# A graph network's edge passes: row numbers kept in place, gathers written out, other rings

## Chip, cores, metric

One core of a Trainium2 chip. The metric is the time of one execution on the device in microseconds; lower is better. Everything is float32.

## What is computed

Four graph layers, one after the other, over 6,250 nodes of 128 features and 100,000 edges. Each layer first takes `h = relu(layernorm(x))` and adds its result to `x`. Cut to what matters:

```python
# first: a message per edge, chosen by its type t of 4, then a GRU over the nodes
h_e = relu([x[src], x[dst]] @ W1[t] + b1[t]);  m = (h_e @ W2[t] + b2[t]) * sigmoid([x[src], x[dst]] @ aw[t] + ab[t])
agg = zeros.at[dst].add(m);  x = layernorm(GRU(agg, x) + x)
# second: attention of every node (row src) over its neighbours (dst)
att = softmax over the edges of a row of (tanh(x)[dst] @ a);  out = segment_sum(tanh(x)[dst] * att, src)
# third: eight bases, mixed by the edge's relation of 64
msg = sum_b w_comp[rel, b] * (x[src] @ weight[b]) * edge_weight;  out = relu(segment_sum(msg, dst) + bias + x @ loop)
# fourth: three graph convolutions
out = segment_sum((x @ W)[src] * norm, dst) + b
```

## The kernel before

**Tables and tiles.** The kernel first sorts the edges by target node (and a second time by source, for the second layer): every edge gets a slot in one of `TILES` = 832 tiles of 128 edges, and all edges of a tile point into one window of 128 nodes (50 windows). A slot holds eight numbers as float32 (`slots`, 128 x tiles x 8): the row of the source node, the rows in the first layer's tables, keys, relation and weight. GpSimd (POOL) scatters them to their slots with indirect DMAs (`Scatter`, L195), and `load_slots` (L669) loads the sorted table into on-chip memory, where it stays.

Each layer then has a table stage, which computes a row per node and stores it in the chip's main memory, and an **edge pass**, which brings the row of each edge's source back and sums over a tile's edges with a matmul against a 0/1 matrix (`onehot`). All passes share one frame. Tiles are handled in groups of `G` = 4, in a ring of `R` = 4 slots (`R1` = 8 in the second layer). `for_groups` (L446) writes out the first turn of the ring, loops over the middle turns (`Fori`), and writes out the last. Each engine runs its own program of this form, and semaphores tie them.

**A gather.** POOL issues one indirect DMA per tile: 128 rows, one per partition, whose numbers are read as int32 from on-chip memory. Since the slots hold floats, ACT first copies the group's numbers into a small int32 ring `index` ("stage"), and POOL waits for it, then issues the group's gathers:

```python
def restage(g, slot, turn):                      # ACT, fourth layer, L1641
    act.wait_ge(q["product"], g + 1)
    stage(g + R, slot)
def gather(g, slot, turn):                       # POOL, L1623
    pool.wait_ge(q["staged"], g + 1)
    pool.sem_inc(q["turns"], 1)
    for j in range(G): pool.indirect_dma_start(...)
```

So the numbers of group g + 4 are staged, and its gathers issued, once PE has done group g's product and the slot is free.

**The passes.** *First layer* (`edges0`, L699): two gathers per tile (L743, tables of 528-byte rows), DVE adds the two rows (L786), ACT makes the message (L766, L769) and then stages (L751), PE multiplies with a 128 x 512 onehot (L846), DVE adds the result into the window's sum (L810); beside it the edge's eight mixing coefficients for the third layer are worked out (L855, L863, L818, L825). *Second layer* (`edges1`, L1075): one gather per tile (L1118), then a running softmax through ACT, PE and DVE four steps deep; ACT stages at the end of `scale_sums` (L1129 called at L1163). Its first staging stands behind the semaphore `cleared`, which DVE raises after clearing the sums (L1176). *Third layer* (`edges2`, L1399): one gather per tile of a 4 KB row, the source's eight products (L1429). ACT scales four of the eight (L1453); DVE scales two in one instruction (L1476), folds two more in one after the other (`chain`, L1488), builds the onehot (L1465), and adds the group before the last into the sums (L1498); PE multiplies the onehot with the six parts left (L1521). ACT's order is: scale group k, then wait for the product of group k - 1 and stage (L1437). DVE's chain of group g waits for the product of group g - 2. *Fourth layer* (`edges3`, L1609), three times: one gather of 512-byte rows per tile (L1628), onehot (L1655), one matmul per tile (L1676), one addition per tile (L1665); ACT does nothing but stage (L1636).

DVE reads the window numbers of a group into registers before its additions (`load_windows_of`, L685).

Of the kernel before, what the change touches and what calls it, by code (L numbers as in the profile page):

```python
# [21 lines left out]
I32 = mybir.dt.int32  # L22
# [21 lines left out]
G, R, R1 = 4, 4, 8  # L44
STEP = G * R1
# [421 lines left out]

def flat(ap):

    return ap.rearrange("p a f -> p (a f)")  # L470
# [198 lines left out]
def load_slots(nc, D, K):  # L669

    with Scope(nc, "slots") as s:
        loaded, cleared = s.sem("loaded"), s.sem("cleared")
# [12 lines left out]
def load_windows_of(nc, K, side, g, before=0):  # L685
# [13 lines left out]
def edges0(nc, A, D, K, acc):  # L699


    with Scope(nc, "edge0") as s:
        index = s.sb("index", [P, R, G, 2], I32)
# [10 lines left out]
        q = {n: s.sem(n) for n in ("loaded", "cleared", "staged", "turns", "summed", "scored", "hidden_done", "onehot_done",  # L714
# [20 lines left out]
        @block.gpsimd  # L735
        def _(pool):
            def gather(g, slot, turn):

                pool.wait_ge(q["staged"], g + 1)
                pool.sem_inc(q["turns"], 1)  # L740
                for j in range(G):
                    for f, (rows, table) in enumerate(((rows_s, "tab_src"), (rows_d, "tab_dst"))):
                        pool.indirect_dma_start(out=rows[:, slot, j, :], out_offset=None, in_=D[table][:, :],  # L743
                                                in_offset=bass.IndirectOffsetOnAxis(ap=index[:, slot, j, f:f + 1], axis=0)).then_inc(gathered[slot], 16)

            for_groups(pool, [(0, gather)])

        @block.scalar
        def _(act):
            def stage(g, slot):  # L750
                act.activation(index[:, slot, :, :], slots[:, ds(g * G, G), F_SRCT:F_DSTT + 1], ACT.Copy).then_inc(q["staged"], 1)  # L751

            for r in range(R):
                stage(r, r)

# [5 lines left out]
            def hide(g, slot, turn):  # L761
# [9 lines left out]

                act.wait_ge(q["hidden_done"], g + 1)
                stage(g + R, slot)
# [301 lines left out]
def edges1(nc, D, K, acc):  # L1075
# [5 lines left out]
    with Scope(nc, "edge1") as s:  # L1081
        slots = s.sb("slots", [P, TP, SF])
        index = s.sb("index", [P, R1, G, 1], I32)
# [16 lines left out]
        q = {n: s.sem(n) for n in ("loaded", "cleared", "staged", "turns", "other_done", "score_done", "score_turned",  # L1100
# [10 lines left out]
        @block.gpsimd  # L1111
        def _(pool):
            def gather(g, slot, turn):

                pool.wait_ge(q["staged"], g + 1)
                pool.sem_inc(q["turns"], 1)
                for j in range(G):
                    pool.indirect_dma_start(out=rows[:, slot, j, :], out_offset=None, in_=D["tab1"][:, :],  # L1118
                                            in_offset=bass.IndirectOffsetOnAxis(ap=index[:, slot, j, 0:1], axis=0)).then_inc(gathered[slot], 16)

            for_groups(pool, [(0, gather)], R1)

        @block.scalar
        def _(act):
            act.wait_ge(q["loaded"], 16)
            act.wait_ge(q["cleared"], 1)

            def stage(g, slot):
                act.activation(index[:, slot, :, :], slots[:, ds(g * G, G), 0:1], ACT.Copy).then_inc(q["staged"], 1)  # L1129

            for r in range(R1):
                stage(r, r)
# [17 lines left out]
            def scale_sums(g, slot, turn):  # L1150
# [11 lines left out]

                stage(g + R1, slot)  # L1163
# [235 lines left out]
def edges2(nc, D, K, acc):  # L1399
# [3 lines left out]

    VB = BASES // 2
    LINKS = 1 + G * (VB - 2)
    PARTS = [0, 1, *range(VB, BASES)]
    with Scope(nc, "edge2") as s:
        index = s.sb("index", [P, R, G, 1], I32)
# [4 lines left out]
        q = {n: s.sem(n) for n in ("loaded", "staged", "turns", "onehot_done", "chain", "scaled", "product", "added")}  # L1413
# [9 lines left out]
        def _(pool):  # L1423
            def gather(g, slot, turn):

# [9 lines left out]
        def _(act):  # L1435
# [3 lines left out]
            for r in range(R):  # L1439
                stage(r, r)  # L1440
# [168 lines left out]
def edges3(nc, D, K, layer, acc):  # L1609

    with Scope(nc, f"edge3_{layer}") as s:
# [22 lines left out]
        def _(act):  # L1634
# [3 lines left out]
            for r in range(R):  # L1638
                stage(r, r)
# [153 lines left out]
```

## Time and profile before

| | us |
|---|---|
| median of 3 timed runs | 11041.12 |
| lowest, highest | 11011.58, 11056.96 |
| span of the profiled execution | 13468.9 |

| stretch of the profiled execution | from, to (us) |
|---|---|
| sorting, first scatters, first tables | 0 to 1775 |
| first layer's edge pass | 1775 to 4664 |
| update, scatters for the second layer | 4664 to 6354 |
| second layer's edge pass | 6354 to 7767 |
| third layer's tables, edge pass | 7767 to 8009, to 9473 |
| fourth layer, three edge passes | 9583 to 10806, 10894 to 12112, 12193 to 13426 |

The page gives each engine's busy time over the span (PE: matmul, PEld: its weight load, DVE, ACT, POOL, SP). A queue name with a q (SPq, ACTq) stands for instructions of an engine's own sequencer, such as register moves, which don't count as busy. POOL's busy time in an indirect DMA is the making of its descriptors; the data move afterwards. "Issue" is idle time in which an engine waited for nothing that the trace shows. A releaser is inferred from semaphore events, and one name may stand for another where a semaphore was used again: in the third and fourth layer "DMA slots_s<-sort_zero" and "DMA tab_dst<-tab_ob" as releaser of DVE and ACT stand for the product's semaphore. The profiled execution took 13,468.9 us; the timed ones are executions of the same program without a profile.

### The profile page before, as it was taken

Reading aid. Unit: us, or ns where it says so; the run is one execution under the profiler, and the core shown is the slowest. Engines: PE = TensorE matmul, PEld = TensorE weight load, DVE = VectorE, ACT = ScalarE, POOL = GpSimd, SP = SyncE. Lnnn points to the kernel's source line nnn. Section 1 sums busy time; section 2 is a strip of 40 time slices with the busy share of each in tenths; the row PEclk is TensorE's granted clock in tenths of the full one; section 3 lists DMA queues with packets and bytes.
Section 4 is the critical chain, followed back from the end, with each engine's and each line's share of the span. In section 5 each row is a group of like instructions: output and inputs, shape, how many; then the busy total and the mean of one; then the engine's idle time right before and its main releaser. Section 6 shows DMA issues by size and latency. Waiting matters only on the chain. (4 is left out here: it accounts for less than half of the span.)

```text
span 13468.9 us, 135567 instructions
## 1 busy us (share of the span) xinstructions
PE 5832.8 (43%) x31462; PEld 5005.1 (37%) x31462; DVE 5298.2 (39%) x11470; ACT 2648.3 (20%) x8918; POOL 7546.1 (56%) x7650
## 2 busy tenths in 40 slices
PE   0003545565565511371444468888433333333332
PEld 0001235555454511251444447787322222222222
DVE  7801034444454400013555546666432332233233
ACT  1000011111111100011555536776200000000000
POOL 2476655655566566406555525555466656665665
PEclk9998567766776755555666689999655555555555
DMA  9901111111111200001111148888211121121112
GB/s 18 13 7 46 51 51 40 41 41 39 40 40 41 36 2 2 1 0 31 39 40 39 39 155 297 298 298 297 79 44 44 45 44 45 45 44 45 45 44 47
DMA packets 587395, 879.08 MB, mean 65 GB/s; under 512 B 340739, under 2 KB 377041, under 8 KB 586828
## 3 DMA queue, kind: packets, MB, share of 16 engines
q0 software_dynamic: 329728, 772.96, 20.9%
q1 hardware_dynamic: 257612, 105.52, 8.7%
q8 instruction: 18, 0.29, 0.0%
q14 instruction: 37, 0.30, 0.0%
HBM read 791.80 MB, written 86.16 MB: 65 GB/s over the span
## 5 line engine op out<-in xcount | busy, mean ns | idle before, releaser
L1628 POOL DMA_INDIRECT edge_rows<-tab,edge_index x2496 | 2399.8, 961 | 1286.1 <-issue 739.4
L1676 PE MATMUL edge_psum<-edge_rows,edge_onehot 128*128 128x128 f32 x4992 | 1250.5, 429 | 2461.3 <-DVE edge_onehot L1655 1434.8
L1676 PEld LDWEIGHTS edge_psum<-edge_rows,edge_onehot 128*128 128x128 f32 x4992 | 1076.8, 318 | 2634.7 <-issue 1507.1
L846 PE MATMUL edge_psum<-edge_hidden,edge_onehot 128*128 128x130 f32 x6656 | 1148.4, 338 | 1297.0 <-DVE acc_acc L810 940.4
L1665 DVE TENSOR_TENSOR acc_acc<-acc_acc,edge_psum 128x128 f32 x2496 | 716.5, 287 | 2514.2 <-remote 1334.2
L846 PEld LDWEIGHTS edge_psum<-edge_hidden,edge_onehot 128*128 128x128 f32 x6656 | 1034.7, 242 | 1416.1 <-DVE acc_acc L810 987.9
L743 POOL DMA_INDIRECT edge_rows_s<-tab_src,edge_index x832 | 842.0, 1012 | 938.6 <-ACT edge_index L751 700.5
L1521 PE MATMUL edge_p_m<-edge_rows,edge_onehot 128*128 128x128 f32 x9984 | 1199.7, 282 | 286.8 <-ACT edge_rows L1453 217.8
L1521 PEld LDWEIGHTS edge_p_m<-edge_rows,edge_onehot 128*128 128x128 f32 x9984 | 1165.8, 197 | 320.7 <-DVE acc_acc L1498 273.6
L1429 POOL DMA_INDIRECT edge_rows<-tab,edge_index x832 | 840.1, 1010 | 639.0 <-ACT edge_index L1437 432.9
L1118 POOL DMA_INDIRECT edge_rows<-tab,edge_index x832 | 797.6, 959 | 626.0 <-ACT edge_index L1129 377.8
L743 POOL DMA_INDIRECT edge_rows_d<-tab_dst,edge_index x832 | 862.4, 1037 | 264.8 <-issue 264.8
L1453 ACT ACTIVATE edge_rows<-edge_rows,edge_coef 128x128 f32<-128x128 f32 x3328 | 996.8, 390 | 33.9 <-issue 17.2
L810 DVE TENSOR_TENSOR acc_acc<-acc_acc,edge_psum 128x520 f32 x832 | 577.7, 694 | 971.7 <-remote 658.1
L1636 ACT ACTIVATE edge_index<-all_slots 128x4 int32 (+1 forms) x636 | 129.0, 208 | 3585.7 <-remote 1664.3
L195 POOL DMA_INDIRECT slots_s<-upd_pay_ring,upd_row_ring x656 | 630.8, 962 | 314.9 <-issue 270.9
L1276 PE MATMUL edge_p_u<-edge_rows,edge_prob 128*128 128x129 f32 x1664 | 375.0, 395 | 751.1 <-ACT edge_prob L1169 511.5
L1276 PEld LDWEIGHTS edge_p_u<-edge_rows,edge_prob 128*128 128x128 f32 x1664 | 319.4, 286 | 819.9 <-ACT edge_prob L1169 507.6
L195 POOL DMA_INDIRECT slots_d<-sort_pay_ring,sort_row_ring x320 | 385.2, 1204 | 257.4 <-DMA sort_pay_ring<-pay_d 158.0
L990 DVE TENSOR_TENSOR upd_new<-upd_rz,upd_p_g 128x128 f32<-128x128 f32 x50 | 14.4, 288 | 1266.1 <-issue 715.6
L195 POOL DMA_INDIRECT slots_d<-tab_pay_ring,tab_row_ring x400 | 384.2, 961 | 226.0 <-issue 143.6
L794 DVE TENSOR_TENSOR edge_onehot<-all_iota,all_slots 128x1024 f32<-128x1024 f32 x416 | 507.6, 1220 | 0.0
(253 smaller groups left out, 9556.9 us busy)
## 6 DMA issues: line engine op xcount, KB each, us to landing
edge_rows<-tab,edge_index POOLq DMA_INDIRECT x4160
tab<-tab_o SPq DMA_DIRECT2D x50, 512.0 KB, 2.6
edge_rows_s<-tab_src,edge_index POOLq DMA_INDIRECT x832
edge_rows_d<-tab_dst,edge_index POOLq DMA_INDIRECT x832
tab_src<-tab_oa SPq DMA_DIRECT2D x50, 264.0 KB
tab_dst<-tab_ob SPq DMA_DIRECT2D x50, 264.0 KB
slots_s<-upd_pay_ring,upd_row_ring POOLq DMA_INDIRECT x656
tab<-acc_own SPq DMA_DIRECT2D x15, 640.0 KB, 3.6
```

The source lines that it names most:

```text
L195: pool.indirect_dma_start(out=self.table[:, :], out_offset=bass.IndirectOffsetOnAxis(ap=self.row_ring[:, z, j:j + 1], axis=0), in_=self.pa ...
L743: pool.indirect_dma_start(out=rows[:, slot, j, :], out_offset=None, in_=D[table][:, :], in_offset=bass.IndirectOffsetOnAxis(ap=index[:, sl ...
L810: v.tensor_tensor(at, at, psum[:, j % 2, :, 0:2 * SW], ALU.add).then_inc(q["added"], 1)
L846: m = pe.matmul(psum[:, j % 2, t // 2, (t % 2) * SW:(t % 2) * SW + SW], onehot[:, slot % 2, j, t * P:(t + 1) * P], hidden[:, slot % 2, j, ...
L1118: pool.indirect_dma_start(out=rows[:, slot, j, :], out_offset=None, in_=D["tab1"][:, :], in_offset=bass.IndirectOffsetOnAxis(ap=index[:, s ...
L1276: m = pe.matmul(p_u[:, z, j // 2, (j % 2) * HW:(j % 2) * HW + H + 1], prob[:, z, j, :], rows[:, slot, j, 0:H + 1], start=True, stop=True)
L1429: pool.indirect_dma_start(out=rows[:, slot, j, :], out_offset=None, in_=D["tab2"][:, :], in_offset=bass.IndirectOffsetOnAxis(ap=index[:, s ...
L1453: a = act.activation(part, part, ACT.Copy, scale=coef[:, ds(G * g + j, 1), b])
L1521: m = pe.matmul(at, onehot[:, z, j, :], rows[:, slot, j, b * H:(b + 1) * H], start=(n == 0), stop=(n == len(PARTS) - 1))
L1628: pool.indirect_dma_start(out=rows[:, slot, j, :], out_offset=None, in_=D[f"tab3_{layer}"][:, :], in_offset=bass.IndirectOffsetOnAxis(ap=i ...
L1665: v.tensor_tensor(at, at, psum[:, slot % 2, j * P:(j + 1) * P], ALU.add).then_inc(q["added"], 1)
L1676: m = pe.matmul(psum[:, slot % 2, j * P:(j + 1) * P], onehot[:, slot % 2, j, :], rows[:, slot, j, :], start=True, stop=True)
```

## The change

1. `load_slots` turns three of the slots' eight fields into int32 **in place**, on DVE, in one instruction each; the second layer's own slots are turned by one ACT instruction. `index` and all staging are gone.
2. A helper `gather_groups` issues all gathers of a pass from a Python loop, so that POOL's program is written out without a loop. Before a group it waits directly for what frees the slot: the message made (first layer), the sums' product (second), the product (third and fourth).
3. The third layer works in groups of two tiles with a ring of eight (same memory); its sums now go two per group.
4. The fourth layer's ring has eight slots of four tiles instead of four. The title's "ring of eight" stands for both.

```diff
+R3 = 8
+G2, R2 = 2, 8
...
+def index_of(slots, field):
+
+
+    return slots[:, 0:TILES, field].bitcast(I32)
+
+
+def gather_groups(pool, ring, freed, gathered, parts, G=G):
+
+
+    for g in range(TILES // G):
+        slot = g % ring
+        wait(pool, freed, g - ring + 1)
+        for j in range(G):
+            for rows, table, slots, field in parts:
+                index = slots[:, G * g + j, field:field + 1].bitcast(I32)
+                pool.indirect_dma_start(out=rows[:, slot, j, :], out_offset=None, in_=table[:, :],
+                                        in_offset=bass.IndirectOffsetOnAxis(ap=index, axis=0)).then_inc(gathered[slot], 16)
...
+            v.wait_ge(loaded, 16)
+            for field in (F_SRC, F_SRCT, F_DSTT):
+                v.tensor_copy(index_of(K["slots"], field), K["slots"][:, 0:TILES, field]).then_inc(indexed, 1)
...
-            for_groups(pool, [(0, gather)])
+            gather_groups(pool, R, q["hidden_done"], gathered,
+                          [(rows_s, D["tab_src"], slots, F_SRCT), (rows_d, D["tab_dst"], slots, F_DSTT)])
...
-                act.wait_ge(q["hidden_done"], g + 1)
-                stage(g + R, slot)
...
-            for_groups(pool, [(0, gather)], R1)
+            pool.wait_ge(q["indexed"], 1)
+            gather_groups(pool, R1, q["sums"], gathered, [(rows, D["tab1"], slots, 0)])
...
+            act.activation(index_of(slots, 0), slots[:, 0:TILES, 0], ACT.Copy).then_inc(q["indexed"], 1)
             act.wait_ge(q["cleared"], 1)
...
-                stage(g + R1, slot)
...
+    G, R, GROUPS = G2, R2, TILES // G2
...
+            gather_groups(pool, R, q["product"], gathered, [(rows, D["tab2"], slots, F_SRC)], G)
...
-            def restage(g, slot, turn):
-
-                act.wait_ge(q["product"], g + 1)
-                stage(g + R, slot)
...
-            for_groups(act, [(0, scale), (1, restage)])
+            for_groups(act, [(0, scale)], R, GROUPS)
...
-                        if sums and (j == 0 or (b, j) == (VB - 1, G // 2)):
+                        if sums and j == 0:
...
-        rows = s.sb("rows", [P, R, G, H])
+        rows = s.sb("rows", [P, R3, G, H])
...
+            gather_groups(pool, R3, q["product"], gathered, [(rows, D[f"tab3_{layer}"], slots, F_SRC)])
...
-            for_groups(v, [(-1, hots), (0, accumulate)])
+            for_groups(v, [(-1, hots), (0, accumulate)], R3)
...
-            "pool_sems": [s.ctx.enter_context(nc.semaphore(f"pool_dma{n}")) for n in range(5 * R + R1)],
+            "pool_sems": [s.ctx.enter_context(nc.semaphore(f"pool_dma{n}")) for n in range(R + R2 + 3 * R3 + R1)],
```

## Rows read from the trace of the kernel before

**Rows 1.** The page: span, and busy time of each engine (share of the span).
```profile
span 13468.9 us, 135567 instructions
...
PE 5832.8 (43%) x31462; PEld 5005.1 (37%) x31462; DVE 5298.2 (39%) x11470; ACT 2648.3 (20%) x8918; POOL 7546.1 (56%) x7650
```

**Rows 2.** Busy time by stretch; columns: us, engines, PEclk, DMA share, GB/s.
```profile
1775.00:4664.00 2889.00, 1626.22 (x9817) 1471.85 (x9818) 1342.59 (x1843) 391.83 (x1439) 1704.36 (x1664) 0.70 0.18 40
...
8009.00:9473.00 1464.00, 1184.72 (x9854) 1151.17 (x9855) 970.64 (x2876) 1018.94 (x3500) 840.11 (x832) 0.97 0.88 299
...
9583.00:10806.00 1223.00, 413.68 (x1648) 356.05 (x1648) 374.52 (x1028) 42.00 (x206) 795.15 (x832) 0.52 0.19 44
```

**Rows 3.** What POOL waited for; columns: us in total, times, longest.
```profile
POOL edge_rows_s L743 <- ACT edge_index L751: 700.5, 77, 19.9
POOL edge_rows L1628 <- ACT edge_index L1636: 546.7, 152, 8.0
...
POOL edge_rows L1429 <- ACT edge_index L1437: 432.9, 193, 16.2
POOL edge_rows L1118 <- ACT edge_index L1129: 377.8, 87, 11.8
```

**Rows 4.** POOL in order of time, fourth layer's first pass; start, us.
```profile
10227.90 0.94 POOL L1628 DMA_INDIRECT edge_rows<-tab,edge_index  x1 [0.30 <-issue]
10229.15 0.94 POOL L1628 DMA_INDIRECT edge_rows<-tab,edge_index  x1 [0.30 <-issue]
...
10236.65 0.94 POOL L1628 DMA_INDIRECT edge_rows<-tab,edge_index  x1 [0.30 <-issue]
10242.11 0.94 POOL L1628 DMA_INDIRECT edge_rows<-tab,edge_index  x1 [4.51 <-ACT edge_index L1636]
```

**Rows 5.** All engines in order of time, the same stretch.
```profile
10224.23 2.07 PE L1676 MATMUL edge_psum<-edge_rows,edge_onehot 128*128 128x128 f32 x8 [3.69 <-DMA edge_rows<-tab,edge_index]
...
10229.40 2.07 PE L1676 MATMUL edge_psum<-edge_rows,edge_onehot 128*128 128x128 f32 x8 [3.10 <-DMA edge_rows<-tab,edge_index]
...
10241.11 1.58 DVE L1665 TENSOR_TENSOR acc_acc<-acc_acc,edge_psum 128x128 f32 x4 [12.15 <-DMA tab_dst<-tab_ob]
10241.11 0.41 ACT L1636 ACTIVATE edge_index<-all_slots 128x4 int32 x2 [14.54 <-DMA tab_dst<-tab_ob]
```

**Rows 6.** Who waited for one line: the fourth layer's table product L1587.
```profile
  DVE acc_own L1604: 62.0, 145
```

**Rows 7.** Line L174 on SP: durations min/median/max in ns.
```profile
L174 SPq MOVE upd_pay_ring<-pay_s x80: 3/700/1400, 4711.1 to 5597.0; - x80
...
L174 SPq MOVE sort_pay_ring<-pay_d x38: 29/29/29, 639.1 to 1017.4; - x38
```

**Rows 8.** All engines in order of time, start of the fourth layer's first pass.
```profile
9581.82 0.50 ACT L1636 ACTIVATE edge_index<-all_slots 128x4 int32<-128x4 f32 x4 [5.99 <-PEq L86]
9582.84 0.98 POOL L1628 DMA_INDIRECT edge_rows<-tab,edge_index  x1 [7.99 <-ACT edge_index L1636]
...
9584.13 0.95 POOL L1628 DMA_INDIRECT edge_rows<-tab,edge_index  x1 [0.31 <-issue]
```

**Rows 9.** The same at the start of the second layer's pass.
```profile
6346.99 5.43 DVE L1176 MEMSET acc_acc<- 128x6450 f32 x1 [1.29 <-issue]
```

**Rows 10.** Groups by line: DVE instructions over 784 numbers.
```profile
L350 DVE SCALAR_TENSOR_TENSOR sort_picked<-sort_win,all_iota,sort_scan 128x784 f32<-128x784 f32 x100 | 103.0, 1031 | 0.1
...
L385 DVE TENSOR_SCALAR sort_mask<-sort_win,all_iota 128x784 f32 x100 | 53.9, 628 | 0.7 <-DVE sort_row L427 0.4 <-DVE sort_payd L380 0.3
```

**Rows 11.** All engines in order of time, third layer, steady stretch.
```profile
8720.99 1.23 DVE L1476 TENSOR_TENSOR edge_rows<-edge_rows,edge_coef 128x1024 f32<-128x1024 f32 x1 [2.30 <-DMA slots_s<-sort_zero]
...
8725.42 0.29 DVE L1498 TENSOR_TENSOR acc_acc<-acc_acc,edge_p_m 128x128 f32 x1
...
8726.14 5.62 PE L1521 MATMUL edge_p_m<-edge_rows,edge_onehot 128*128 128x128 f32 x48 [1.36 <-ACT edge_rows L1453]
...
8735.06 1.22 DVE L1476 TENSOR_TENSOR edge_rows<-edge_rows,edge_coef 128x1024 f32<-128x1024 f32 x1 [2.41 <-DMA slots_s<-sort_zero]
```

More of the change, by code:

```diff
@@ L1412, in edges2 @@
         p_m = s.ps("p_m", [P, 2, 512])
-        q = {n: s.sem(n) for n in ("loaded", "staged", "turns", "onehot_done", "chain", "scaled", "product", "added")}
+        q = {n: s.sem(n) for n in ("loaded", "onehot_done", "chain", "scaled", "product", "added")}
         gathered = [K["pool_sems"].pop() for _ in range(R)]
@@ L1423, in _ @@
         def _(pool):
-            def gather(g, slot, turn):
-                pool.wait_ge(q["staged"], g + 1)
-                pool.sem_inc(q["turns"], 1)
-                for j in range(G):
-                    pool.indirect_dma_start(out=rows[:, slot, j, :], out_offset=None, in_=D["tab2"][:, :],
-                                            in_offset=bass.IndirectOffsetOnAxis(ap=index[:, slot, j, 0:1], axis=0)).then_inc(gathered[slot], 16)
-            for_groups(pool, [(0, gather)])
+            gather_groups(pool, R, q["product"], gathered, [(rows, D["tab2"], slots, F_SRC)], G)
         @block.scalar
         def _(act):
-            def stage(g, slot):
-                act.activation(index[:, slot, :, :], slots[:, ds(g * G, G), F_SRC:F_SRC + 1], ACT.Copy).then_inc(q["staged"], 1)
-            for r in range(R):
-                stage(r, r)
             act.wait_ge(q["loaded"], 16)
-            def restage(g, slot, turn):
-                act.wait_ge(q["product"], g + 1)
-                stage(g + R, slot)
             def scale(g, slot, turn):
@@ L1522, in products @@
                 m.then_inc(q["product"], 1)
[L1524 removed]
+            for_groups(pe, [(0, products)], R, GROUPS)
 def finish2(nc, A, D, K, acc):
@@ L1611, in edges3 @@
     with Scope(nc, f"edge3_{layer}") as s:
[L1612 to L1613 removed]
+        rows = s.sb("rows", [P, R3, G, H])
         onehot = s.sb("onehot", [P, 2, G, P])
         psum = s.ps("psum", [P, 2, 512])
[L1616 to L1617 removed]
+        q = {n: s.sem(n) for n in ("cleared", "onehot_done", "product", "added")}
+        gathered = [K["pool_sems"].pop() for _ in range(R3)]
         block = s.block()
@@ L1622, in _ @@
         def _(pool):
-            def gather(g, slot, turn):
-                pool.wait_ge(q["staged"], g + 1)
-                pool.sem_inc(q["turns"], 1)
-                for j in range(G):
-                    pool.indirect_dma_start(out=rows[:, slot, j, :], out_offset=None, in_=D[f"tab3_{layer}"][:, :],
-                                            in_offset=bass.IndirectOffsetOnAxis(ap=index[:, slot, j, 0:1], axis=0)).then_inc(gathered[slot], 16)
-            for_groups(pool, [(0, gather)])
-        @block.scalar
-        def _(act):
-            def stage(g, slot):
-                act.activation(index[:, slot, :, :], slots[:, ds(g * G, G), F_SRC:F_SRC + 1], ACT.Copy).then_inc(q["staged"], 1)
-            for r in range(R):
-                stage(r, r)
-            def restage(g, slot, turn):
-                act.wait_ge(q["product"], g + 1)
-                stage(g + R, slot)
-            for_groups(act, [(0, restage)])
+            gather_groups(pool, R3, q["product"], gathered, [(rows, D[f"tab3_{layer}"], slots, F_SRC)])
         @block.vector
```

44 lines of the change are left out of this document (8 added, 36 removed).

## The prediction, made before the change was run

> **What bounds the kernel now.** I began with the page [rows 1]. No engine is full: POOL leads with 56% of a 13,468.9 us span, and PE follows with 43%. A share over the span says little here, so the second view was busy time by stretch [rows 2]. It shows the edge passes, which the change touches: the first layer's 2,889 us, the third's 1,464, and of the fourth's three passes the first took 1,223. In the first and fourth layer POOL is the busiest engine, DMA is busy for a fifth of the time, and the only thing POOL does is issue gathers; so it is in the second, which has no row. In the third layer 299 GB/s keep DMA busy for 0.88, and PE works 1,185 us.
>
> Third, what POOL waits for [rows 3]. The change touches one kind of wait: POOL idle until ACT had staged the row numbers, 700.5 us in 77 waits (first layer), 377.8 in 87 (second), 432.9 in 193 (third), 546.7 in 152 (fourth). Beside it stands POOL's own beat: in a steady stretch a gather takes 0.94 us, with 0.30 us of "issue" before it [rows 4], 1.25 from one to the next. A pass of 832 gathers can't be shorter than 832 x 1.25 = 1,040 us, and the first (1,664) not than 2,080. The waits sum to 2,057.9 us in 509; each holds the 0.30 us that is there anyway, which leaves 1,905.
>
> Now the step on which all hangs. The timed runs have a median of 11,041.12 us, and the profiled execution's span is 13,468.9: 2,428 us longer. The sum below is made against that execution, but a saving there counts only if the timed runs have it too. Take all 1,905 us of waits out of the span and 11,564 is left, still 523 above the median. So recording lengthens something by at least that. Two things are large enough: the waits (1,905), or the 0.30 us before each of 5,824 gathers and 1,568 scatters (784 columns, twice): 2,218.
>
> What do the rows say of that? In a fourth-layer wait POOL stops after the gather of 10236.65 and goes on at 10242.11 [rows 4]. PE had issued a product at 10224.23 and another at 10229.40, each modelled 2.07 us, but DVE and ACT go on only at 10241.11, 14.8 us after the first one's modelled end [rows 5]; products are added in order, and these are the first one's additions. PE has nothing to do in that time and no data are missing for it: the word that it is done comes late. In the table stages, where POOL gathers nothing, a product's reader has waited 62.0 us in 145 waits, 0.4 us each [rows 6]. And a register move of SP takes 29 ns in one stage and a median of 700 ns in another, at the same line [rows 7]; such an instruction has no operand to wait for. I read this as records being written late and holding up PE, DVE and SP. What is certain is only that slow passages strike instructions that do no work.
>
> The Trainium skill allows this: "NOTIFIC — the notification-queue block", section 7.1, says that the block's internal pipeline pushes back on producers rather than lose a record, so that tracing can throttle an engine. If so, the waits are the recording's. No run here shows an engine without its records.
>
> **The change part by part.** (a) Per group, ACT's staging and its hop go, and POOL waits on the product itself. Where POOL is held by its own beat, this frees nothing; the cover is POOL's beat. Where waits are real it gives the hop: ACT at 10241.11, POOL at 10242.11, 1.0 us. The slot waits otherwise stay where they were in the first layer (ring of four) and the second (eight, but released by the product instead of by ACT's scaling of the sums). ACT was not a bound in any pass.
>
> (b) Written-out gathers. A loop's back edge falls between the gathers of 10227.90 and 10229.15 [rows 4]: 1.25 us apart, as everywhere. So nothing is gained there. POOL's 5,824 gathers become straight-line code and must be fetched. The first turns of a pass, written out already, keep the same beat [rows 8]: 0 us. The Trainium skill, "Runtime: NRT & Kernel Launch", section on instruction fetch, says that a taken branch can break the prefetch and that straight-line code is streamed. By that rule each back edge would cost something today and the change would win it, at no price that the page gives; the trace disagrees, with the usual 0.30 us at a back edge, and by it the sum gets 0.
>
> (c) Start of a pass: ACT stages at 9581.82, POOL starts at 9582.84 [rows 8]. Five passes begin about 1 us earlier, -5. In the second layer ACT's staging, and so POOL, stood behind DVE's clearing of the sums, 5.43 us [rows 9]; it now stands behind the slots' load alone. Between 0 and -5.4, taken -2.
>
> (d) Three conversions of 832 numbers on DVE after the slots' load. Nearest are 784 numbers at 628 ns and, strided products, at 1,031 [rows 10]. Between 1.9 and 3.1 us, taken 2.7.
>
> (e) The fourth layer's ring of eight: POOL may run 32 gathers ahead, 40 us, instead of 16, 20 us. Covers the 14.8 us lateness with room; takes away nearly all of 546.7 - 152 x 0.30 = 501 us in the profiled execution, and 0 where the lateness isn't there.
>
> (f) The third layer in pairs. Its beat is 7.0 us per four tiles [rows 11]. One round of the two-group loop: DVE starts at 8720.99, its last addition ends at 8725.71, PE starts at 8726.14, works 5.62 to 8731.76, and DVE starts again at 8735.06. That is 14.07 us for two groups: 10.34 of work that scales with tiles and 3.73 that is fixed. In pairs the work per group halves and the fixed part doesn't. If all 3.73 are real, four tiles take 5.17 + 3.73 = 8.9, so (8.9 - 7.03) x 208 = +389 us. If only the 0.43 from DVE to PE and 0.2 more are real, it was PE-bound at 5.62 and becomes 5.17 + 0.63 = 5.8: +37. And if data bind (299 GB/s at 0.88 busy is 340 GB/s, 2.1 MB per four tiles, 6.17 us) both hide: 0. Below: the 2 us by which POOL idles per group might be what holds it, and the floor of 5.62 would give (5.62 - 7.03) x 208 = -293. I take +18, between the two readings that go with undisturbed signals, because the timed runs have no room for the disturbed ones.
>
> Sum: -5 - 2 + 2.7 + 18 = +14, thus **11,055 us**. (About 0.5%, 55 us, is what a measurement of this kernel can tell from nothing.)
>
> **The rivals.**
> - **No change** (the above): POOL keeps its beat, and the waits belong to the recording. For: the median. Against: the gap of 0.30 us could be the recording's instead. Its own range is 10,990 to 11,110. Chance 0.46.
> - **The waits are real, the beat is shorter without records.** Then (e) gives up to 501 us, the hops 77 + 87 of about 1 us and an earlier release in the second layer another 150 or so: 11,041 - 600 = 10,440 at most. If a third to a half of the waits is real, 10,750 to 10,840. For: 2,218 us of gaps explain the difference as well. Against: register moves of 700 ns. Chance 0.33, mostly in its smaller form.
> - **Slower through pairs in the third layer.** Place: the loop product, DVE chain, product. Price up to +389, so 11,430; it decides from a fixed part over about 1.3 us per group (5.17 + 1.3 = 6.47, 0.3 above the data's 6.17, times 208 = 60 us). For: the fixed part of 3.73 was measured. Against: most of it is lateness after PE's modelled end. Chance 0.18.
> - **It doesn't do what it says**: the waits move from ACT's staging to the product's semaphore, as long as before. The time is as in the first case; chance 0.03 beside it.
>
> **How the numbers follow.** Faster is the second case and a little of the first: 0.34. Slower is the third and the upper edge of the first: 0.20. The rest is 0.46. The range leaves out the fullest form of the second (below 10,650) and of the third (above 11,230).
>
> **What would show it.** In the changed profile: gathers at 1.25 us still; waits of POOL in the fourth layer down from 546.7 us to under 150, the first layer's about as before (its ring is the same), so a span hundreds of us shorter; the third pass at 1,300 to 1,700 us. I am wrong if the timed median falls by more than 55 us while the gathers' beat stays 1.25, or if it rises with the third pass. A profiled span that falls by 500 us beside an unmoved median would be the clearest sign that the reading is right.

## The result, and the profile after

The changed kernel takes 11,050.47 us (median of 20 runs, 11,030.05 to 11,078.97), the kernel before 11,017.15 us (20 runs, 10,998.92 to 11,056.96) beside it: a ratio of 1.0028, interval 1.002 to 1.0036. So it is slower by 33 us, 0.3%. The profile of the changed kernel, first the page:

```profile
span 11047.8 us, 131181 instructions
...
PE 5766.2 (52%) x31462; PEld 4948.5 (45%) x31462; DVE 5348.3 (48%) x11889; ACT 2422.0 (22%) x7643; POOL 7559.0 (68%) x7650
...
q14 instruction: 80, 0.66, 0.0%
```

Against [rows 1] the span is 2,421 us shorter, while each engine's busy time is nearly the same (but for ACT's, 226 us less). Busy time by stretch, the stretches of [rows 2] (first layer, third, one pass of the fourth):

```profile
1632.00:3945.00 2313.00, 1575.59 (x9913) 1478.31 (x9913) 1348.06 (x1861) 329.87 (x1244) 1805.57 (x1664) 0.80 0.23 50
6339.00:7590.00 1251.00, 1191.37 (x9955) 1145.25 (x9956) 1044.33 (x3323) 1018.07 (x3328) 801.65 (x832) 0.99 0.96 352
7684.00:8730.00 1046.00, 425.65 (x1647) 366.60 (x1648) 367.80 (x1028) 0.00 (x0) 790.84 (x832) 0.50 0.22 52
```

The first layer's pass went from 2,889 us to 2,313, one of the fourth's from 1,223 to 1,046, and the third layer runs with DMA 0.96 busy instead of 0.88. What POOL waited for (total us, times, longest), which answers to [rows 3], and POOL in order of time in a fourth-layer pass, which answers to [rows 4]:

```profile
POOL edge_rows L485 <- issue: 1143.8, 3748, 0.5
POOL edge_rows L485 <- PE edge_p_m L1494: 300.2, 401, 1.5
...
POOL edge_rows_s L485 <- issue: 253.3, 831, 0.3
```
```profile
8202.50 0.94 POOL L485 DMA_INDIRECT edge_rows<-tab,all_slots  x1 [0.30 <-issue]
8203.75 0.94 POOL L485 DMA_INDIRECT edge_rows<-tab,all_slots  x1 [0.30 <-issue]
8205.00 0.94 POOL L485 DMA_INDIRECT edge_rows<-tab,all_slots  x1 [0.30 <-issue]
```

The gather still costs 0.94 us and the 0.30 before it is still there, 1.25 together. The waits of 700.5, 377.8 and 546.7 us are gone; 300.2 us remain, all in the third layer, behind its product L1494. The start of a fourth-layer pass [rows 8] and the conversions [rows 10]:

```profile
7684.37 0.97 POOL L485 DMA_INDIRECT edge_rows<-tab,all_slots  x1 [7.51 <-ACTq L86]
...
7685.65 0.95 POOL L485 DMA_INDIRECT edge_rows<-tab,all_slots  x1 [0.31 <-issue]
```
```profile
L701 DVE CAST all_slots<-all_slots 128x832 int32<-128x832 f32 x3 | 2.5, 905 | 10.3 <-DMA all_slots<-slots_d 10.3
```

And the line that proved to be the key, SP's register moves (min/median/max ns), which stood at 3/700/1400 in [rows 7]:

```profile
L176 SPq MOVE upd_pay_ring<-pay_s x80: 29/29/29, 3980.2 to 4787.2; - x80
```

A span 2,421 us shorter beside a median 33 us longer can't be the change's doing. Which part is the change's, and which isn't, is what the experiments ask.

### The profile page after: what moved, and what is told of

The parts are those of the page before. It is cut to its first block and busy times, and to the rows that moved or that the text cites. A ratio compares the mean times of both kernels' runs of the same rounds, so it can differ in the third digit from the quotient of the medians.

```text
span 11047.8 us, 131181 instructions
## 1 busy us (share of the span) xinstructions
PE 5766.2 (52%) x31462; PEld 4948.5 (45%) x31462; DVE 5348.3 (48%) x11889; ACT 2422.0 (22%) x7643; POOL 7559.0 (68%) x7650
## 5 line engine op out<-in xcount | busy, mean ns | idle before, releaser
L485 POOL DMA_INDIRECT edge_rows<-tab,all_slots x3328 | 3171.7, 953 | 1230.8 <-issue 890.5
L1625 PE MATMUL edge_psum<-edge_rows,edge_onehot 128*128 128x128 f32 x4992 | 1291.1, 440 | 1899.8 <-DMA edge_rows<-tab,all_slots 1688.9
L852 PEld LDWEIGHTS edge_psum<-edge_hidden,edge_onehot 128*128 128x128 f32 x6656 | 1111.8, 262 | 868.7 <-DVE acc_acc L816 758.5
L1494 PE MATMUL edge_p_m<-edge_rows,edge_onehot 128*128 128x128 f32 x9984 | 1195.0, 279 | 65.5 <-DVE edge_rows L1461 40.5
L1494 PEld LDWEIGHTS edge_p_m<-edge_rows,edge_onehot 128*128 128x128 f32 x9984 | 1148.6, 192 | 111.9 <-issue 95.6
L485 POOL DMA_INDIRECT edge_rows_d<-tab_dst,all_slots x832 | 957.8, 1151 | 253.5 <-issue 253.5
L485 POOL DMA_INDIRECT edge_rows_s<-tab_src,all_slots x832 | 847.9, 1019 | 275.2 <-issue 253.3
L485 POOL DMA_INDIRECT edge_rows<-tab,edge_slots x832 | 810.6, 974 | 261.9 <-issue 253.3
L1569 ACT ACTIVATE tab_hT<-tab_p_t 128x128 f32<-128x128 f32 x150 | 41.4, 277 | 2268.5 <-PE tab_p_t L1555 2266.3
L1461 DVE SCALAR_TENSOR_TENSOR edge_rows<-edge_rows,edge_coef 128x128 f32<-128x128 f32 x1664 | 511.5, 348 | 0.0
L775 ACT ACTIVATE edge_hidden<-edge_rows_s 128x4 f32<-128x4 f32 x208 | 43.7, 210 | 1979.7 <-DVE edge_rows_s L792 1979.7
L792 DVE TENSOR_TENSOR edge_rows_s<-edge_rows_s,edge_rows_d 128x528 f32<-128x528 f32 x208 | 149.7, 720 | 657.0 <-DMA edge_rows_d<-tab_dst,all_slots 657.0
```

The lines of the kernel that those rows point to most:

```text
L792: v.tensor_tensor(rows_s[:, slot, :, :], rows_s[:, slot, :, :], rows_d[:, slot, :, :], ALU.add).then_inc(q["summed"], 1)
L852: m = pe.matmul(psum[:, j % 2, t // 2, (t % 2) * SW:(t % 2) * SW + SW], onehot[:, slot % 2, j, t * P:(t + 1) * P], hidden[:, slot % 2, j, ...
L1461: v.scalar_tensor_tensor(first, rows[:, slot, j, b * H:(b + 1) * H], coef[:, ds(G * g + j, 1), b], first, ALU.mult, ALU.add).then_inc(q["c ...
L1494: m = pe.matmul(at, onehot[:, z, j, :], rows[:, slot, j, b * H:(b + 1) * H], start=(n == 0), stop=(n == len(PARTS) - 1))
L1625: m = pe.matmul(psum[:, slot % 2, j * P:(j + 1) * P], onehot[:, slot % 2, j, :], rows[:, slot, j, :], start=True, stop=True)
```

## The experiments

All ratios are to the kernel before on the same chip. "Pass" is the stretch from a pass's first gather to its last.

### The kernel before once more, and three halves of the change

**before_again** is the kernel before without an edit.

> The kernel before, unchanged, profiled once more. Theory A (POOL's waits for the staged numbers belong to the first recording, POOL's own beat holds the timed runs): where the recording is not disturbed, the span comes to about 11,020 us, as the timed runs, the fourth layer's passes to 1,040 to 1,050 us each with a beat of 1.25 us, and POOL's waits for ACT there to under 20 us instead of 546.7. Theory B (the waits are part of the kernel and the change took them away, while something else took their place): the waits come again, 300 us or more in the fourth layer. Time against the kernel before: 1.000.

**no_pairs** is the whole change but for the pairs:

```diff
-G2, R2 = 2, 8
+G2, R2 = 4, 4
...
-                        if sums and j == 0:
+                        if sums and (j == 0 or (b, j) == (VB - 1, G // 2)):
```

> The changed kernel with the third layer back in groups of four tiles in four slots. If the pairs cost the 33 us by which the changed kernel is slower (theory P), the time returns to about 11,017 us, ratio 1.000, and the third layer's pass is some 30 us shorter than the changed kernel's 1,234. If the cost lies elsewhere (theory W: written-out code, conversions), the ratio stays at 1.002 to 1.004.

**pairs_alone** is the kernel before with nothing but the pairs, the numbers still staged by ACT:

```diff
+G2, R2 = 2, 8
...
+    G, R, GROUPS = G2, R2, TILES // G2
...
-            for_groups(act, [(0, scale), (1, restage)])
+            for_groups(act, [(0, scale), (1, restage)], R, GROUPS)
...
-                        if sums and (j == 0 or (b, j) == (VB - 1, G // 2)):
+                        if sums and j == 0:
```

> The kernel before with only the third layer in groups of two tiles and a ring of eight; loops and staging stay. Theory P: +30 us or more, ratio 1.003 or above, since staging through ACT adds to the loop of product and chain. Theory W: within 10 us of the kernel before, since data bind that pass at 350 GB/s either way.

**ring_alone** is the kernel before with nothing but the fourth layer's ring:

```diff
+R3 = 8
...
-        index = s.sb("index", [P, R, G, 1], I32)
-        rows = s.sb("rows", [P, R, G, H])
+        index = s.sb("index", [P, R3, G, 1], I32)
+        rows = s.sb("rows", [P, R3, G, H])
```

> The kernel before with only the fourth layer's ring at eight slots. Theory A: nothing, within 5 us, since POOL does not wait there in the timed runs. Theory B: 100 us or more faster, since the ring covers the waits.

Measured, before at 11,048.98 us:

| kernel | us | ratio, interval | span | third pass, us |
|---|---|---|---|---|
| before_again | 11,047.68 | 1.000, 0.9991 to 1.001 | 11,035.8 | 1,202 |
| no_pairs | 10,996.02 | 0.9954, 0.994 to 0.9967 | 10,993.3 | 1,148 |
| pairs_alone | 11,116.48 | 1.006, 1.0046 to 1.0074 | 11,122.0 | 1,271 |
| ring_alone | 11,052.76 | 1.0001, 0.9992 to 1.001 | 11,057.9 | 1,201 |

The first line alone takes the ground from under [rows 1]: the same program has a span of 11,035.8 us here and 13,468.9 there, so theory A is right that the waits belong to the first recording. Recording them isn't what made them: 11,035.8 us recorded lies within 0.2% of the median. pairs_alone bears out theory P (+67 us) and refutes W. no_pairs bears out that the pairs cost, but neither of its theories has the size: P asked for a ratio of 1.000 and a pass some 30 us shorter, and it is 0.9954 and 85 us, because P took the hop to be free. Its fourth-layer pass, and SP's moves:

```profile
7675.00:8717.00 1042.00, 424.33 (x1640) 365.09 (x1640) 374.58 (x1028) 42.67 (x205) 788.77 (x832) 0.50 0.22 52
```
```profile
L174 SPq MOVE upd_pay_ring<-pay_s x80: 29/29/29, 3996.0 to 4803.0; - x80
```

In this recording the pass is at 832 x 1.25 = 1,040 us, so there is nothing for a ring of eight to win, and ring_alone wins nothing. The third passes, by stretch (after, before_again, no_pairs, pairs_alone, in this order):

```profile
6339.00:7572.00 1233.00, 1173.49 (x9804) 1127.98 (x9805) 1028.75 (x3272) 1008.28 (x3296) 800.51 (x831) 0.99 0.97 354
```
```profile
6358.00:7560.00 1202.00, 1133.22 (x9836) 1110.80 (x9837) 968.99 (x2870) 1021.07 (x3495) 876.67 (x831) 0.99 0.98 363
```
```profile
6354.00:7502.00 1148.00, 1112.17 (x9828) 1104.08 (x9829) 973.18 (x2866) 983.23 (x3288) 831.13 (x831) 0.99 1.00 380
```
```profile
6366.00:7637.00 1271.00, 1150.24 (x9810) 1112.54 (x9811) 1021.41 (x3275) 1060.52 (x3687) 835.87 (x831) 0.99 0.95 344
```

Nearly the whole change lies here (the first layer's pass differs by 14 us, the second's and the fourth's by about 2). Without the staging hop the pass falls by 54 us (1,202 to 1,148), and the pairs add 85 (1,148 to 1,233), or 69 with the hop kept (1,202 to 1,271). 85 - 54 = +31 us is the +33 of the result. In no_pairs the DMA engines are busy all the time, 1.00, at 380 GB/s, and pairs take the pass away from that: 0.97, 354 GB/s. TensorE is nearly full as well in no_pairs, 1,112 of 1,148 us; which of the two holds the pass there was not separated on this kind of chip.

Where the hop costs is to be seen in before_again, third layer, in order of time:

```profile
7005.65 0.21 ACT L1437 ACTIVATE edge_index<-all_slots 128x4 int32 x1 [1.14 <-PE edge_p_m L1521]
7006.66 0.94 POOL L1429 DMA_INDIRECT edge_rows<-tab,edge_index  x1 [1.08 <-ACT edge_index L1437]
```

ACT stages 1.01 us before POOL can gather. The sum of such waits is no price, though. before_again has 83.0 us in 73 of them, of which 16.3 us stand before the pass's first gather; no_pairs has 100.3 us in 127 behind the product itself and is 54 us faster. What the hop costs shows in those who use the rows: VectorE's waits for data, and TensorE's for the parts that ScalarE scales, both up to the pass's last product, before_again and then no_pairs:

```profile
DVE edge_rows L1476 <- DMA edge_rows<-tab,edge_index: 206.9, 169, 21.1
PE edge_p_m L1521 <- ACT edge_rows L1453: 65.0, 63, 26.9
```
```profile
DVE edge_rows L1449 <- DMA edge_rows<-tab,all_slots: 94.1, 72, 20.4
PE edge_p_m L1494 <- ACT edge_rows L1426: 37.8, 19, 26.2
```

VectorE waits less for rows, and ScalarE, which no longer waits for a product before it scales, holds TensorE up less often. no_pairs takes away both the hop and ScalarE's wait; which of them gives how much of the 54 us was not separated on this kind of chip.

Where the pairs cost is to be seen in the waits of VectorE in the third pass, no_pairs and then after:

```profile
DVE edge_rows L1449 <- PE edge_p_m L1494: 89.9, 136, 4.1
DVE edge_rows L1449 <- DMA edge_rows<-tab,all_slots: 89.3, 70, 20.4
```
```profile
DVE edge_rows L1449 <- PE edge_p_m L1494: 175.4, 359, 3.5
DVE edge_rows L1449 <- DMA edge_rows<-tab,all_slots: 18.5, 2, 18.1
```

With fours VectorE waits for data and for TensorE alike. With pairs it hardly waits for data; it waits 359 times for TensorE's product of two pairs ago, and its own work has grown by 55.6 us (973.18 to 1,028.75), in 406 more instructions. The data aren't early for all that: ScalarE, which scales as soon as the rows are there, waits for them longer and more often, no_pairs and then after:

```profile
ACT edge_rows L1426 <- DMA edge_rows<-tab,all_slots: 169.4, 206, 20.6
```
```profile
ACT edge_rows L1426 <- DMA edge_rows<-tab,all_slots: 221.6, 308, 18.4
```

One round in after, order of time:

```profile
7002.55 0.75 DVE L1449 TENSOR_TENSOR edge_rows<-edge_rows,edge_coef 128x512 f32<-128x512 f32 x1 [0.53 <-PE edge_p_m L1494]
7002.57 0.94 POOL L485 DMA_INDIRECT edge_rows<-tab,all_slots  x1 [1.01 <-PE edge_p_m L1494]
...
7005.36 0.94 POOL L485 DMA_INDIRECT edge_rows<-tab,all_slots  x1 [0.60 <-PE edge_p_m L1494]
7005.43 0.69 DVE L1449 TENSOR_TENSOR edge_rows<-edge_rows,edge_coef 128x512 f32<-128x512 f32 x1 [0.31 <-PE edge_p_m L1494]
```

VectorE and POOL are let go by the same product, once per pair, and the transfers into the freed slot start only then.

### Four kernels that fell on another kind of chip

The next four were to split these two effects further. Their chip turned out to be one on which the kernel before takes 13,512 us in its timed runs too. They are of use all the same, since [rows 1 to 11] look like theirs.

**act_waits** is no_pairs, with ACT given back its wait and a copy for which nobody waits:

```diff
+        spare = s.sb("spare", [P, 2, G, 1], I32)
...
+            def restage(g, slot, turn):
+                act.wait_ge(q["product"], g + 1)
+                act.activation(spare[:, slot % 2, :, :], slots[:, ds(g * G, G), F_KEY:F_KEY + 1], ACT.Copy).then_inc(q["restaged"], 1)
...
-            for_groups(act, [(0, scale)], R, GROUPS)
+            for_groups(act, [(0, scale), (1, restage)], R, GROUPS)
```

> The third layer's pass in groups of four with the direct wait took 1148 us from first to last gather, with the hop through ScalarE 1203. This kernel keeps the direct wait of GpSimd, and gives ScalarE back its wait for each group's product and one small copy of four columns per group (208 of them), for which nobody waits. Theory A (the hop delays the gathers: GpSimd hears of a free slot only when ScalarE has scaled the group after it): the pass stays at 1148 us, the whole at about 10,996. Theory B (ScalarE, held up by the wait for the product, scales late and TensorE with it): the pass returns to about 1200 us, the whole to about 11,047. 208 copies of about 0.25 us each on ScalarE alone, if they all lay on the path, would be the same 52 us, so ScalarE's waits for its gathers (174.1 us of idle time in that kernel) have to be read beside it: if they stay above 100 us, the copies were covered.

**rest_alone** is the changed kernel with `edges2` as before, but its staging reads the resident integers:

```diff
-        gather_groups(pool, R, q["product"], gathered, [(rows, D["tab2"], slots, F_SRC)], G)
...
+        for_groups(pool, [(0, gather)])
...
+        act.activation(index[:, slot, :, :], slots[:, ds(g * G, G), F_SRC:F_SRC + 1].bitcast(I32), ACT.Copy).then_inc(q["staged"], 1)
```

> The changed kernel everywhere except in the third layer, where the edge pass is the earlier one: groups of four, four slots, each group's numbers copied by ScalarE (now from the resident integers). If the third layer holds both effects (direct wait about -55 us, pairs about +86), this kernel is at the earlier kernel's time, 11,049 us within 10, with a third pass of about 1203 us. If resident numbers and written-out gathers gave part of the 53 us in the other layers, it is faster than that by that part: at 11,020 half of it would be outside the third layer.

**deep_pairs** is the changed kernel with four buffers for sums and one-hots:

```diff
-        onehot = s.sb("onehot", [P, 2, G, P])
-        p_m = s.ps("p_m", [P, 2, 512])
+        onehot = s.sb("onehot", [P, 4, G, P])
+        p_m = s.ps("p_m", [P, 4, 512])
...
-                    v.wait_ge(q["product"], g - 1)
+                    v.wait_ge(q["product"], g - 2)
...
-                wait(pe, q["added"], G * (g - 1))
+                wait(pe, q["added"], G * (g - 3))
```

> The changed kernel with pairs, but four PSUM and four one-hot buffers instead of two, the additions three pairs behind the chain instead of two, TensorE allowed four pairs ahead of them. Theory C (pairs halve the distance in time between the product and the addition that waits for it, so VectorE waits for TensorE at each pair: 177.9 us in 365 waits in the changed kernel, against 89.9 in 136 with fours): those waits shrink below 60 us, and the third pass falls from 1234 us to between 1150 and 1190, the whole to 10,970 to 11,005. Theory D (what pairs cost is the extra 208 groups themselves: their fixed parts on VectorE, and the semaphores between engines): the pass stays within 15 us of 1234 and the whole within 15 of 11,050, and the waits of VectorE move to another releaser.

**light_fours** is no_pairs with less to do for TensorE and ScalarE:

```diff
-                    for b in range(VB, BASES):
+                    for b in range(VB, VB + 1):
...
+    LIGHT = [0, 1]
...
-                    for n, b in enumerate(PARTS):
+                    for n, b in enumerate(LIGHT):
```

> Groups of four with the direct wait, and less work in the third layer's pass: TensorE multiplies two of the six parts, ScalarE scales one of the four bases; VectorE's work and the gathers are kept. The output of the layer lacks those bases. If the transfers set the pass at 1148 us (5.52 us per four tiles, 379 to 386 GB/s), it stays above 1130. If TensorE's 24 products per group (48 matmul columns' worth at 112 ns, 5.38 us) set it, it falls to the next limit: GpSimd's 1.249 us per gather would give 1039, VectorE's row of operations lies between.

Measured, before at 13,512.07 us (third pass and fourth-layer pass of before from the first recording, 13,468.9 us):

| kernel | us | ratio, interval | third pass | a fourth-layer pass |
|---|---|---|---|---|
| before | 13,512.07 | | 1,461 | 1,222 |
| rest_alone | 13,165.75 | 0.9745, 0.9715 to 0.9775 | 1,465 | 1,192 |
| act_waits | 13,045.64 | 0.9661, 0.9631 to 0.969 | 1,345 | 1,191 |
| deep_pairs | 13,000.56 | 0.963, 0.9599 to 0.9662 | 1,323 | 1,191 |
| light_fours | 12,970.54 | 0.9604, 0.9572 to 0.9637 | 1,254 | 1,191 |

Timed, not only recorded: the long waits belong to this kind of chip. SP's moves in rest_alone show the mark:

```profile
L176 SPq MOVE upd_pay_ring<-pay_s x80: 3/1062/1422, 4625.4 to 5514.5; - x80
```

**rest_alone** was expected at the time of before; there it would have decided whether the other layers gain. On this chip they do: from first to last gather the first layer's pass goes from 2,887 us to 2,811, the second's from 1,411 to 1,271, the fourth's three from 3,659 to 3,575, and the third stays. That is 300 us of the 346. What POOL waited for in the second layer's pass, before and then rest_alone, shows one of them:

```profile
POOL edge_rows L1118 <- ACT edge_index L1129: 377.8, 87, 11.8
```
```profile
POOL edge_rows L485 <- PE edge_p_u L1267: 133.1, 56, 5.2
POOL edge_rows L485 <- DMA sort_pay_ring<-pay_d: 103.9, 53, 5.6
```

POOL waits on one thing only there, the sums' product; the second line is the same wait under another name. So 377.8 us in 87 waits became 237.0 in 109. Whether it is the hop, the loop of POOL or the ring (this in the fourth layer) that gives these 300 us, rest_alone doesn't say, as it changes all of them.

In one fourth-layer pass the waits shrink little, before and then rest_alone:

```profile
POOL edge_rows L1628 <- ACT edge_index L1636: 188.8, 52, 8.0
```
```profile
POOL edge_rows L485 <- remote: 148.2, 53, 4.9
```

A ring twice as long leaves three quarters of them: the chain of products and additions behind the gathers comes to a stop as well, and a longer lead doesn't make it catch up. (That this is why was not tried by itself.)

**act_waits** against rest_alone is the direct wait in the third layer, with ACT held up as before: 1,465 to 1,345 us, ratio down by 0.0084. So the gain doesn't need ScalarE to be free of its wait, and theory A has the better of it; what that wait costs beside it isn't known, as no_pairs did not run here. But the two differ in written-out gathers as well. They changed no beat on the first kind; here, in the trace's semaphore events, TensorE's update comes a median of 3.0 us after the modelled end of a product in rest_alone and 1.7 in act_waits. Whether the hop or that lateness gave the 120 us was not tried. **light_fours** says how far the transfers go here:

```profile
7806.00:9151.00 1345.00, 1154.48 (x9840) 1116.64 (x9840) 979.24 (x2876) 1020.79 (x3500) 838.52 (x831) 0.99 0.93 325
```
```profile
7802.00:9056.00 1254.00, 655.87 (x3280) 604.97 (x3280) 984.06 (x2865) 263.19 (x824) 908.19 (x831) 0.68 0.96 348
```

act_waits first, light_fours second: with TensorE's work down to 656 us the pass still takes 1,254, with DMA 0.96 busy. By the letter of the expectation (above 1,130 us) transfers are the limit, though its figures were those of the other kind of chip; GpSimd's 1,039 was far from reached. But 90 us did go, with TensorE's and ScalarE's work and with ScalarE's extra wait, and in light_fours TensorE waits 384.0 us for VectorE's additions and 184.5 for its chain, while VectorE, 984 us busy, waits 81.8 us for data. So transfers have a part in the limit; how large it is was not shown.

### Four repeats, to find the first kind of chip again

> The same kernel as deep_pairs, which ran on a chip where the earlier kernel takes 13,512 us, so that its pass (1323 us) has nothing to stand beside. On a chip where the earlier kernel takes about 11,049 us: theory C (pairs halve the distance between a product and the addition that waits for it) gives a third pass of 1150 to 1190 us and a ratio of 0.993 to 0.997; theory D (what pairs cost is the 208 further groups themselves) gives 1234 us within 15 and a ratio of 1.000 to 1.003. On a chip of the other kind it repeats 0.963.

> The same kernel as act_waits. On the other chip its third pass took 1345 us, 120 less than that of rest_alone with the hop through ScalarE, 1465. On a chip where the earlier kernel takes about 11,049 us: theory A (the hop delays the gathers) gives a pass of 1148 us and a ratio of 0.995; theory B (ScalarE held up by the product) gives about 1200 us and a ratio of 1.000.

> The changed kernel itself, for a time on the chip where the earlier kernel takes about 13,510 us and its profile looks like the one the prediction rests on (TensorE's semaphore updates up to 14 us late wherever GpSimd issues indirect transfers). There rest_alone took 13,166 us (ratio 0.9745), act_waits 13,046, deep_pairs 13,001 to 13,037. The prediction's sum of -501 us for the fourth layer's ring holds there only if the waits of 546.7 us go away: the passes of the fourth layer already read 1191 us instead of about 1220, so the ring brings 28 us for each of three, about 84, and not 501. With pairs as slow as on the other chip the whole lies at 13,050 to 13,120 us (ratio 0.966 to 0.971); if pairs cost nothing there, at 13,000 to 13,040. If this run falls on the other kind of chip it repeats 1.000 to 1.004.

> The kernel of deep_pairs once more, since both of its runs fell on chips where the earlier kernel takes 13,510 us. On a chip where the earlier kernel takes 11,050 to 11,080 us and the changed kernel's third pass 1233 us (after and after_b): theory C (pairs halve the distance between a product and the addition that waits for it, and VectorE's 177.9 us of waiting for TensorE is the price) gives a third pass of 1150 to 1190 us, VectorE's waits for TensorE there below 60 us, and a ratio of 0.993 to 0.997; theory D (the 208 further groups cost by themselves) gives 1234 us within 15 and a ratio of 1.000 to 1.004.

| kernel | us | before there | ratio, interval | third pass |
|---|---|---|---|---|
| deep_pairs_b | 13,037.25 | 13,515.01 | 0.9641, 0.9609 to 0.9674 | 1,323 |
| act_waits_b | 13,067.61 | 13,515.01 | 0.9661, 0.9629 to 0.9693 | 1,344 |
| after_b | 11,104.10 | 11,078.52 | 1.0025, 1.0015 to 1.0036 | 1,233 |
| deep_pairs_c | 12,904.39 | 13,360.15 | 0.9668, 0.9637 to 0.970 | 1,297 |

after_b confirms the result, and the third pass of 1,233 us with it. deep_pairs never met that kind of chip, and the changed kernel as it is never met the other. So theory C (too short a distance between product and addition) against theory D (the 208 further groups by themselves) stays open. Two things on record bear on it. On the other kind of chip pairs with the deeper buffers are no slower than fours: deep_pairs takes 1,323 us for the third pass and 13,001 for the whole, act_waits on the same chip 1,345 and 13,046, and the repeats 1,323 and 13,037 against 1,344 and 13,068 (act_waits has ScalarE's extra wait, though). That leans to C, but VectorE still waits 223 us for TensorE in deep_pairs (150.2 and 72.9, under two names), where C had asked for less than 60. And VectorE's 55.6 us more of work is D's: deep_pairs_c keeps it, 1,038.63 us, 59 more than act_waits:

```profile
7716.00:9013.00 1297.00, 1168.45 (x9821) 1125.94 (x9822) 1038.63 (x3281) 1008.26 (x3296) 825.46 (x832) 0.99 0.94 337
```

How much of the 85 us it is that reaches the end of the pass isn't known.

## Why the prediction was right, and where it wasn't

The time (11,050 against 11,055) and the size of the effect (+33 against +14 us, so no change by the 0.5% bound) came out within the first case's own range. That the sum came so near is luck in part: two of its terms were wrong by 54 and 67 us, with opposite signs. Its steps fared unequally.

- **That the waits count for nothing in the timed runs** was right for the chips on which the result was timed; **its reason was wrong**. "I read this as records being written late" fell with before_again (recorded, 11,035.8 us, no such waits) and with 11 timed runs of before at 13,512 us. The waits, and SP's moves, go with the chip. The gap of 2,428 us between span and median was the gap between two chips, so "recording lengthens something by at least that" fails as well. The rule cited from the Trainium skill ("NOTIFIC — the notification-queue block", section 7.1) isn't needed for any of it, and no run here shows such a throttle. And the "clearest sign", a span that falls by hundreds of us beside an unmoved median, did appear and proved nothing: it would have appeared without any change.
- **Rival two** wanted real waits and a shorter beat without records. The beat is 1.25 us in every recording, and a first-layer pass can't be under 2,080 us. The waits are real, but on the other kind of chip; there kernels with parts of this change have ratios of 0.960 to 0.975.
- **(a) the hop, 0**: right in the second and fourth layer (passes within about 2 us of before_again's) and near in the first (14 us less), failed in the third. The prediction measured the hop at 1.0 us and let it fall with the long waits; it is there between short waits as well, and removing it, with ScalarE's wait, gives -54 us.
- **(b) written-out gathers, 0**: the same 1.25 us, and 80 packets of instructions where the kernel before has 37, with no gap before a gather. The page of the Trainium skill cited there ("Runtime: NRT & Kernel Launch", section on instruction fetch) speaks of a branch whose target isn't among the instructions already held, which the prediction left out. So a back edge at the usual beat doesn't contradict it, and no run here tries a longer loop.
- **(c) and (d), -7 and +2.7**: the conversions took 2.5 us. POOL's idle time before a fourth-layer pass is 7.51 us where it was 7.99 [rows 8]: half a us saved per pass, not one. ACT's and POOL's start in the second layer now stand at 5039.16 and 5040.39, inside the clearing of the sums that POOL waited out before [rows 9]:

```profile
5036.37 5.43 DVE L1167 MEMSET acc_acc<- 128x6450 f32 x1 [1.29 <-issue]
5039.16 0.95 ACT L1124 ACTIVATE edge_slots<-edge_slots 128x832 int32<-128x832 f32 x1 [110.84 <-DMA edge_slots<-slots_s]
5040.39 0.97 POOL L485 DMA_INDIRECT edge_rows<-tab,edge_slots  x1 [8.68 <-ACT edge_slots L1124]
```

- **(e) the ring of eight, 0 timed, -501 in the profiled execution**: 0 is right (ring_alone, 1.0001). The 501 was over-sized: on that kind of chip the three passes give 84 us together (rest_alone), and that with the hop and the loop gone too. The step that failed is "Covers the 14.8 us lateness with room": a fourth-layer pass keeps 148.2 us of waits of its 188.8. That a lead covers one late product, but not a chain that stands still with it, is the likely reason, not a tested one.
- **(f) the pairs, +18**: the mis-sized term. It measured +85. The +18 was the mean of two readings. One, +37, had 5.8 us per four tiles against 5.62 before; measured are 5.93 (1,233 / 208) with pairs and 5.52 (1,148 / 208) with fours, so 0.41 and not 0.18. The other, 0, had the data hide both, with a floor of 6.17 us from a recording at 299 GB/s; at 380 GB/s it is at most 5.52 and hides nothing. The +18 came out near the net effect only because the missing -54 of (a) made up for it, which was luck. The sum with the measured sizes, the -7 of (c) left as forecast: -54 + 85 + 2.5 - 7 = +27, against 33 measured.
- **Rival three**, the loop of product and chain, was the right place for the loss, at about a fifth of its full price of 389 us: most of the 3.73 us of fixed part was the lateness on the first recording's chip (a median of 3.0 us after a product's modelled end there, 0.01 in before_again), as its sentence against it said.
- **The signs**: the beat of 1.25 us and the fourth layer's waits under 150 us came as announced. Two did not: the first layer's waits, expected "about as before", are gone too, and the third pass, put at 1,300 to 1,700 us, takes 1,233. Both were read off the recording of the other kind of chip.

The faster version is no_pairs, 0.9954: the change without its pairs, 0.5% faster than the kernel before and 0.7% than the changed one. On the other kind of chip it wasn't run; act_waits, which is no_pairs and a little more, has 0.9661 there.

## What to carry to other kernels

Before a wait is costed from one recording, hold that recording's span against the timed runs; where they differ by more than a per cent, the profile is of another machine than the median, and the first thing to buy is the unchanged kernel's profile again. In a pass whose transfers keep DMA full, the time from a product to the next gather is on the path: take out a hop there (-54 us here), but don't halve the groups, which adds a wait and some fixed work per group (+85 here). And a sum may come out right by two errors of opposite sign; only runs with one part each show it.

## What the hardware showed that was not expected

- **Two kinds of chip.** The same program takes 11,017 to 11,079 us on one kind and 13,360 to 13,515 on the other. One chip was met twice and was of the first kind both times, three others were of the second; whether it is the chip itself or what surrounds it, no run tells. On the latter SP's register moves take a median of 700 to 1,062 ns (29 otherwise), and in the trace's semaphore events TensorE's updates come a median of 3.0 us after the modelled end of the third layer's products in before and rest_alone, and 1.7 us in act_waits and deep_pairs_c (0.01 in before_again and after). The granted clock, 0.67 to 0.69 on average against 0.71, doesn't explain it: in the third pass both kinds have 0.97 or more, and the pass takes 1,461 and 1,202 us. What does is open.
- **Gathers of 4 KB rows at 380 GB/s** on one core, DMA share 1.00 (no_pairs), where the first recording gave 299.
- **The first layer's pass keeps a loss of its own**: 1,664 x 1.249 = 2,078 us would do, it takes 2,311 with and 2,325 without the change (after, before_again), through gathers that last longer than 0.94 us. That, 230 us or so, is the largest loss these passes have left, and no run here was about it.
